# Reading du back from DRAM ahead of the step sizes, in a Mamba layer with a feed-forward network

## The reference

```
delta = softplus(dt_lo @ dt_proj_w.T + dt_proj_b)          # the step sizes
dA = exp(delta_t * A)
h  = dA * h + (delta_t * u_t) * b_t                         # du = delta * u
y_t = sum over the 16 states of h * c_t
```

## Time and profile before

| | us |
|---|---|
| median of 3 runs | 3186.46 |
| the runs | 3184.78 to 3187.3 |
| the profiled execution's own time | 3178.26 |
| its span, first to last instruction | 3176.2 |
| DVE busy over the whole span | 2349.8 (74%) |
| DMA queue q1 (SP), share of 16 engines over the span | 34.1% |
| DMA queue q10 (ACT), the same | 10.4% |

### The profile page before, as it was taken

The page is one execution under the profiler, slowest core; times in us unless marked ns, Lnnn a source line. Parts: engine busy times, 40 slices in busy tenths (PEclk is TensorE's granted clock), DMA queues, the critical chain, the costliest instruction groups (busy, mean ns, idle before and its releaser), DMA issues. The chain is left out here.

```text
span 3176.2 us, 39976 instructions
## 1 busy us (share of the span) xinstructions
PE 2726.6 (86%) x10900; PEld 1623.3 (51%) x10900; DVE 2349.8 (74%) x2845; ACT 2006.5 (63%) x3326; POOL 1758.9 (55%) x902
## 2 busy tenths in 40 slices
PE   5787887887888888888888975589999999999997
PEld 2243333343333333333333432378888888888886
DVE  2999989999999899999999999634544445444442
ACT  3767767777767767777677776554555554555542
POOL 0898898898899898899898899400000000000000
PEclk8788988888888888989888887799999999999998
DMA  4465466466465464565555655652222222222210
GB/s 135 101 183 148 127 172 160 117 183 159 114 192 156 118 192 125 147 176 130 159 154 130 180 147 141 226 177 74 76 89 73 73 86 66 89 83 66 92 40 14
DMA packets 236286, 402.54 MB, mean 127 GB/s; under 512 B 22976, under 2 KB 62144, under 8 KB 236096
## 3 DMA queue, kind: packets, MB, share of 16 engines
q1 hardware_dynamic: 174336, 293.48, 34.1%
q10 hardware_dynamic: 61760, 106.98, 10.4%
HBM read 276.12 MB, written 124.26 MB: 126 GB/s over the span
## 5 line engine op out<-in xcount | busy, mean ns | idle before, releaser
L1181 DVE TENSOR_TENSOR_SCAN h<-bank,state,db 128x512 f32<-128x512 f32 x1024 | 1252.7, 1265 | 47.9 <-POOL hc L1044 27.0
L1044 POOL TENSOR_TENSOR hc<-h,c_rows 128x1024 f32<-128x1024 f32 x512 | 1201.0, 2374 | 29.9 <-PE bank L634 22.8
L863 ACT ACTIVATE bank<-d_bc,a_neg 128x512 f32<-128x512 f32 x1024 | 691.2, 685 | 383.5 <-DVE h L1181 285.8
L1165 DVE TENSOR_TENSOR db<-bank,du_bc 128x2048 f32<-128x2048 f32 x192 | 435.5, 2268 | 71.1 <-DMA du_bc<-du_rows 71.1
L1523 ACT ACTIVATE s_h<-s_bank,sc 128x512 f32<-128x512 f32 x256 | 175.9, 687 | 493.1 <-PE s_bank L1462 492.8
L1462 PE MATMUL s_bank<-s_mid,h_r 128*128 128x512 f32 x2048 | 467.0, 389 | 0.0
L703 PE MATMUL bank<-x_t,w 128*128 128x512 f32 x1024 | 384.0, 504 | 63.9 <-ACT ab L933 31.0
L1462 PEld LDWEIGHTS s_bank<-s_mid,h_r 128*128 128x128 f32 x2048 | 384.5, 188 | 80.1
L613 PE MATMUL bank<-bc,w_spread 64*128 64x512 f32 x272 | 155.1, 579 | 260.9 <-DVE db L1165 257.2
L1055 POOL TENSOR_TENSOR db<-du_bc,b_row 128x2048 f32<-128x2048 f32 x64 | 291.3, 4551 | 143.5 <-DVE h L1181 137.5
L634 PE MATMUL bank<-hc,fold_w 128*32 128x512 f32 x2048 | 338.1, 739 | 10.9 <-POOL hc L1044 6.6
(11 more groups left out here) (140 smaller groups left out, 3602.6 us busy)
## 6 DMA issues: line engine op xcount, KB each, us to landing
ab<-ab ACTq DMA_DIRECT2D x264, 256.0 KB, 4.2
d_bc<-d_rows SPq DMA_DIRECT2D x256, 256.0 KB, 4.8
du_bc<-du_rows SPq DMA_DIRECT2D x256, 256.0 KB, 7.8
s_abr<-ab SPq DMA_DIRECT2D x120, 512.0 KB, 3.7
w<-w ACTq DMA_DIRECT2D x128, 256.0 KB, 3.8
d_rows<-sp_r SPq DMA_DIRECT2D x64, 256.0 KB, 2.0
du_rows<-sp_w SPq DMA_DIRECT2D x64, 256.0 KB, 2.0
x<-res SPq DMA_DIRECT2D x17, 512.0 KB, 9.0
```

The source lines that it names most:

```text
L863: act.activation(decays[DECAY_BANK[g]][:], d_bc[c % 2][:, j, :], ACT.Exp, scale=a_neg[:, g:g + 1]).then_inc(decay, 1)
L1044: pool.tensor_tensor(hc[:, k % HCSTEPS, at:at + HG], h[:, H_SLOT[k], at:at + HG], c_rows[:, q, :].unsqueeze(1).broadcast_to([P, HG, NT]), ...
L1165: dve.tensor_tensor(db[:, k % DBSTEPS], p_b[:].unsqueeze(1).broadcast_to([P, JC, NT]), du_bc[c % 2][:], ALU.mult).then_inc(db_dve, 1)
L1181: dve.tensor_tensor_scan(h[:, H_SLOT[k], j, :], decays[DECAY_BANK[g]][:], db[:, k % DBSTEPS, j, :], state[:, g:g + 1], ALU.mult, ALU.add). ...
```

## The change

In `copies` the two blocks that read back change places: the waits on `db_dve`, `db_pool` and `du_out[k]` and the four transfers into `du_bc[k]` now stand ahead of the waits on `decay` and `d_out[k]` and the four transfers into `d_bc[k]`. The two writes to DRAM stay ahead of both. No instruction is added or taken away.

```diff
                 sp.wait_ge(du, t.count(KI, c + 1))
                 sp.dma_start(du_rows[k], sp_w[k][:]).then_inc(du_out[k], 16)
 
-                sp.wait_ge(decay, t.count(NG, GC * (c - 1) + DECAY0))
-                sp.sem_inc(waited, 1)
-                sp.wait_ge(d_out[k], t.count(32, 16 * (c // 2 + 1)))
-                for nn in range(GN):
-                    sp.dma_start(d_bc[k][nn * GD:(nn + 1) * GD, :, :],
-                                 d_rows[k].rearrange("(j d) t -> d j t", d=GD)).then_inc(d_in[k], 16)
-
                 sp.wait_ge(db_dve, t.count(KI * QV, QV * (c - 1) + DVE0))
                 sp.sem_inc(waited, 1)
                 sp.wait_ge(db_pool, t.count(KI, c - 1 + POOL0))
@@
                 for nn in range(GN):
                     sp.dma_start(du_bc[k][nn * GD:(nn + 1) * GD, :, :],
                                  du_rows[k].rearrange("(j d) t -> d j t", d=GD)).then_inc(du_in[k], 16)
+
+                sp.wait_ge(decay, t.count(NG, GC * (c - 1) + DECAY0))
+                sp.sem_inc(waited, 1)
+                sp.wait_ge(d_out[k], t.count(32, 16 * (c // 2 + 1)))
+                for nn in range(GN):
+                    sp.dma_start(d_bc[k][nn * GD:(nn + 1) * GD, :, :],
+                                 d_rows[k].rearrange("(j d) t -> d j t", d=GD)).then_inc(d_in[k], 16)
```

## The result

The changed kernel takes 3135.62 us (median of 4 runs, 3133.17 to 3145.36) where the kernel before took 3185.62 beside it (4 runs, 3184.26 to 3187.3). The ratio is 0.9851, with a 95% interval of 0.9838 to 0.9863: 50 us less. In a later round of runs the same pair gave 3136.75 against 3179.02, ratio 0.9857 (0.9835 to 0.9879). The profiled execution went from its own 3178.26 us to 3133.98, 44.3 less; its span from 3176.2 to 3131.2. The first stage alone ends 43.8 earlier (DVE's L1253, the first instruction of the second stage, starts at 1965.1, not 2008.9).

What follows compares the result with a forecast made beforehand. The prediction took DVE's work plus its gaps to bound the first stage, the largest gap being du_bc waits. Gains of 36.3 (chunk 3), 12.2 (chunk 1) and 1.4 (opening) made 49.9 us, giving 3137 us, own range 3129 to 3146.

Steps and rivals of the forecast that it cites:

- The places and the queue: DVE's du waits stand at chunks 3 and 1; first megabyte takes 7.1 us, two 12.0, so du lands 3.5 earlier.
- All 22 waits: DVE's waits for du_bc outside the opening, 54.3 us: sixteen at chunk 3 (40.1), six at chunk 1 (14.2); all can go.
- d's reads moved back: d_bc lands 6.2 us later at chunk 3, still in time for ACT's exponentials, with 3.0 us margin, about 1.4 in the tightest.
- POOL gives back 3.8: Behind chunk 3, POOL's idle time limits the gain: 3.8 of 40.1 us returns as DVE's wait for hc.
- ACT, charged 2 us at chunk 1 (0 to 8): Late d_bc makes ACT slip at the three longest chunk 1 waits: 2 us charged, between nothing and 8.
- comes earlier with them: PE, which stood 257 us for DVE's products, comes earlier when those products do; no size given.
- The opening, 1.4: At the kernel's start du lands earlier and d at 76.4; first scan moves from 78.65 to about 77.2, gaining 1.4 us.
- The sum: 36.3 us at chunk 3, 12.2 at chunk 1, 1.4 in the opening: 49.9 us gained; chance 0.62.
- A shorter shift: Rival: du's landing moves only 1.8 us earlier, so waits shrink but stay, 36 us gained, 3150; chance 0.12.
- no effect: Rival: transfers share engines and end together, du 1.3 us later, 3215, or the waits stay as they are; chance 0.03.
- d in du's place: Rival: at chunk 3 exponentials start late because d_bc is now second, and the scan stands for ACT, 3213; chance 0.06.
- ACT takes most of it: Rival, POOL or ACT: chunk 3's gain returns as waits for hc and exponentials, leaving 13.6 us, 3173; chance 0.15.

Runs made afterwards that it cites:

- the two kernels with a gate: Chunk 0's second set of reads waits for the m = 3 w12 load: du's on the kernel before, 3166.24 us; d's on the changed kernel, 3123.20 us.
- the gate alone: Kernel before, order unchanged, but chunk 0's du reads wait until the w12 load for m = 3 has landed: 3166.24 us against 3182.84, ratio 0.9946.
- Chunk 1 alone: Kernel before with du's reads put first at chunk 1 only: 3164.29 us against 3179.02, ratio 0.9948.
- chunk 3 alone: Kernel before with du's reads first at chunk 3 only: 3173.95 us against 3179.02; with chunk 0's du reads held for w12, 3133.55 against 3182.84.

## Why the prediction was right, and where it was not

- *The places and the queue.* Right in each step. All 22 waits went. One megabyte took 7.0 us and two 12.1 where 7.1 and 12.0 were worked out. The figure of the Trainium skill (DMA: Bandwidth & Descriptors, section Bandwidth), by which the prediction had estimated a shift of 1.8 us instead of 3.5, would have left waits that are not there. The run with a quarter of d's bytes shows the cause. One reading was too kind: 14.9 us for two megabytes was the worst chunk 1 by its wait, but two others took 15.4 and 16.3.
- *d's reads moved back.* Nearly right. Four waits of ACT for d_bc, 6.2 us in all, are new beside the opening. The run with one d read first, which took nearly all of them away, gave no time, but it had more waits elsewhere.
- *POOL gives back 3.8.* Not seen: DVE's wait for hc went from 27.0 to 24.4, and between the two kernels with a gate from 29.8 to 28.9. "Behind the chunk 1 waits POOL idles 4 to 5 us" was also misread: behind the largest, 5.04, it idled 2.13.
- *ACT, charged 2 us at chunk 1 (0 to 8).* Here the sum was mis-sized. DVE's waits for ACT grew by 22.2 us, 2.3 of them in the opening, and for the most part not for d. The step that failed is the sentence that PE "comes earlier with them", which was given no price: against chunk 0's write of delta, the load of m = 3 is issued 2.5 us earlier (7.9 behind it before, 5.4 after, means of 15 tiles), and PE's product comes as much earlier. But w12 lands with those of chunk 0's reads that are ahead of it. These start when POOL has made delta. Chunk 0's write of delta is 22.2 or 22.3 us behind chunk 3's in both kernels (medians), although DVE no longer waits there, and in the new order the reads begin and end 1.3 later. Where six or more are ahead, the load lands some 15 us behind that write, as in the kernel before, and PE's wait grows by about what PE is early. The prediction also took PE's waits for w12 in the kernel before as costing nothing; the gate alone says otherwise.
- *The opening, 1.4.* It gave 0: d landed at 77.9, not 76.4.
- *The sum.* 49.9 forecast; 50.0 by the first medians, 42.3 by the second, 44.3 in the profiled executions. The forecast is inside this scatter, and luck has a part in it. Outside the opening ACT's waits cost 18 us more than the 2 charged; against that, hc cost 3.8 + 2.6 = 6.4 less than charged and PE's folded result 4.1 less. The profiled execution gained 5.6 less than forecast. Where w12 is out of the way, chunk 3 and chunk 1 together are worth 43 of the forecast's 48.5. Chunk 1 alone is worth 15 without a gate, chunk 3 alone 33 with it and 5 without, where I had 12 and 36.
- *The rivals.* A shorter shift, no effect, and d in du's place are excluded by the rows of the landing. "ACT takes most of it" was the nearest to what happened, by a mechanism that it did not name.

Open: how much of the loss is the lower clock and how much the wait for w12 itself. No run changed one without the other. The traces say that both count. In chunk 3 alone a wait of 3.87 us was followed by a granted clock of 0.66 for 5 us and 1.00 for the next 5, and DVE then waited 3.6 us for ACT in all; one of 3.81, followed by 0.50 for 10 us, had 5.5 behind it. Low clock without a long wait cost little: behind a wait of 1.45 us in the kernel before the clock was 0.68 and then 0.50, and DVE waited 0.4. That the order of chunk 0's reads is what makes chunk 3 alone lose so much rests on the count of reads ahead, in one profiled execution of each kernel.

## What to carry to other kernels

Here a transfer on the critical path was timed by the bytes ahead of it in its queue: put first what is read first, and count that the other set moves back by the whole of what passes it. Then look at who else has a transfer in flight there, on other queues too, and count how many large transfers are issued ahead of each small one. A small load that is nearly in time becomes a longer wait once its reader comes earlier. Holding back a large set that has slack, by one semaphore, was worth 11 to 14 us on the changed kernel and 17 on the kernel before.

## What the runs showed that was not expected

With six of SP's reads issued ahead, a 64 KB load took 6.9 to 7.4 us and a 256 KB load 8.3 to 9.2; with at most five ahead a 256 KB load took 4.0 to 7.3, but for one of 8.4. After PE's 3.74 us wait for one the granted clock was 0.50 for the next 10 us, while behind a wait of 1.35 us four products took 1.19 us at full clock; but one of 3.87 was followed by full clock after 5 us. Fifteen waits for w12, 37.0 us in PE's own row, had no more than 0.2 us of DVE's waits for ACT behind each of them. And two edits of order in one tile did not add up: 5 us and 17 us apart, 49 together.
